# Reciprocal roots on GpSimd, a variance from the first moments, and two of a batch's query/key products one iteration earlier

## What is computed

```
x = x + Attn(norm(x))            # 16 heads of 32; softmax(q k^T); product with Wff, plus bff
x = x + CrossAttn(ctx, norm(x))  # one head of 512 over 750 context rows
h = norm(x); x = x + gate * agg  # agg: 8 best of 2048 keys, softmax, weighted sum of gathered rows
norm(x) = (x - mean) / sqrt(var + 1e-5)
v    = var of the normalised rows h;   lv = log1p(v)
gate = sigmoid(gwc * clip(0.5 * lv / mean(lv) + 2.5 * sigmoid(mlp(h)), 0, 5) + gbc)
```

## Time and profile before

| | |
|---|---|
| time, median of 3 runs | 2811.0 us (2810.16 to 2812.33) |
| profiled execution: span from first to last instruction | 2786.2 us |
| the profiled execution's own time | not given beside its span; the runs' median is 24.8 us above it |
| PE busy, share of the span | 2556.4 us, 92% |
| DVE, ACT, POOL busy | 77%, 51%, 25% |
| TensorE's granted clock, mean over the span | 0.971 |
| loads and stores of HBM | 358.87 MB, mean 129 GB/s |

### The profile page before, as it was taken

How to read it: one execution, slowest core, us unless ns; L and a number is a source line. 1 busy time by engine, 2 the same in 40 slices (tenths; PEclk the granted TensorE clock), 3 DMA queues, 4 the chain that set the end, 5 groups by cost and what they waited for, 6 DMA issues and landing times.

```text
span 2786.2 us, 56938 instructions
## 1 busy us (share of the span) xinstructions
PE 2556.4 (92%) x19090; PEld 2104.0 (76%) x19090; DVE 2146.0 (77%) x4207; ACT 1431.3 (51%) x4247; POOL 683.1 (25%) x650
## 2 busy tenths in 40 slices
PE   6899999999999999999999999999999999999730
PEld 4578878887888788878887888778888887788520
DVE  5456888888888888888888888888888888887552
ACT  2345554555555545555555455555554555555252
POOL 0001222222222222222222222222222222222254
PEclk9899999999999999999999999999999999999955
DMA  5223354454544444444444445444445454444799
GB/s 189 53 80 80 107 132 121 128 137 130 133 121 112 130 125 123 138 131 131 128 111 128 131 113 138 131 131 131 115 126 134 106 139 130 132 130 111 202 205 178
DMA packets 131542, 358.87 MB, mean 129 GB/s; under 512 B 21906, under 2 KB 26514, under 8 KB 123267
## 3 DMA queue, kind: packets, MB, share of 16 engines
q0 software_dynamic: 63520, 160.60, 24.4%
q1 hardware_dynamic: 63188, 192.15, 23.6%
q10 hardware_dynamic: 4784, 5.46, 0.6%
HBM read 316.37 MB, written 41.78 MB: 129 GB/s over the span
## 4 chain that ended last, share of the span: by engine, by line
PE 74%; DVE 8%; ACT 7%; issue 7%; DMA 2%; POOL 1%; DVEq 0%; ACTq 0%; POOLq 0%; SPq 0%
PE psX L1144 43%; PE psA L1144 13%; PE psA L1153 5%; PE psF L1144 4%; PE psA L1210 4%; DVE top L999 3%; PE psA L1233 2%; ACT paT L640 2%; PE psX L1153 2%; ACT sc L640 1%; DMA vg<-in_L_ffn_aux_values,idx 1%; ACT xT_hi L663 1%; DVE xmax L948 1%; PE psF L1153 1%; DVE idx L1002 1%
## 5 line engine op out<-in xcount | busy, mean ns | idle before, releaser
L589 POOL DMA_INDIRECT vg<-in_L_ffn_aux_values,idx x512 | 491.7, 960 | 1550.5 <-DVE agg L1028 1053.8
L684 ACT ACTIVATE pa<-psA,nmax 112x224 f32<-112x224 f32 x1024 | 444.6, 450 | 197.8 <-DVE nmax L917 194.5
L917 DVE TENSOR_REDUCE nmax<-psA 112x4 f32<-112x896 f32 x256 | 267.1, 1085 | 100.9 <-PE psA L1210 100.9
L1144 PE MATMUL psX<-big,gT 128*112 128x375 f32 x1024 | 333.4, 478 | 0.6 <-ACT gT L711 0.6
L1028 DVE SCALAR_TENSOR_TENSOR agg<-vg,wt,agg 112x512 f32<-112x512 f32 x406 | 303.8, 748 | 9.2
L1144 PE MATMUL psX<-pT,cx 125*128 125x224 f32 x1536 | 299.1, 355 | 0.0
L1144 PEld LDWEIGHTS psX<-pT,cx 125*128 125x128 f32 x1536 | 288.0, 190 | 4.0 <-issue 0.3
L932 DVE TENSOR_TENSOR pa<-pa,rsum 112x896 f32<-112x896 f32 x256 | 279.4, 1091 | 8.8
L1144 PEld LDWEIGHTS psX<-big,gT 128*112 128x112 f32 x1024 | 175.2, 176 | 126.0 <-issue 0.9
L1153 PE MATMUL psA<-ident,pa 112*112 112x112 f32 x2048 | 227.2, 262 | 19.5 <-DVE oT_lo L895 19.4
L640 ACT COPY paT<-psA 112x448 f32<-112x448 f32 x512 | 237.2, 560 | 11.4 <-PE psA L1153 9.4
(11 more groups left out here) (220 smaller groups left out, 5957.0 us busy)
## 6 DMA issues: line engine op xcount, KB each, us to landing
big<-in_ctx_t SPq DMA_DIRECT2D x32, 1500.0 KB, 8.1
cx<-in_ctx SPq DMA_DIRECT2D x32, 1344.0 KB
xa<-in_x SPq DMA_DIRECT2D x64, 224.0 KB
centered<-in_x_t SPq DMA_DIRECT2D x32, 448.0 KB, 4.6
x<-in_L_attn_bff POOLq DMA_DIRECT2D x32, 448.0 KB, 5.7
x<-cb_scratch POOLq DMA_DIRECT2D x32, 448.0 KB, 5.9
x<-in_x SPq DMA_DIRECT2D x31, 448.0 KB
out<-x SPq DMA_DIRECT2D x30, 448.0 KB, 3.1
```

Source lines behind the costliest of these rows:

```text
L589: pool.indirect_dma_start(vg[:, c % SLOTS, k, :], None, aux_values, bass.IndirectOffsetOnAxis(ap=idx[:, t, n:n + 1], axis=0))\
L684: last = nc.scalar.activation(pa[:, t, h, :], psA[0:R, h, t * S:(t + 1) * S], ACT.Exp, bias=nmax[:, k % 2, h, t:t + 1], accum_out=rsum[:, ...
L917: nc.vector.tensor_reduce(nmax[:, k % 2, h:h + 2, :], psA[0:R, h:h + 2, 0:T * S].rearrange("p h (t s) -> p h t s", t=T), AX_X, ALU.max, ne ...
L1144: last = nc.tensor.matmul(dst, stationary, moving, start=n == 0, stop=n == len(pairs) - 1)
```

## The change

Four edits, of which only the order of steps touches TensorE.

1. Roots. The seed and the three Newton rounds are gone from VectorE. A new step `root`, right after the new step `stat`, lets GpSimd raise `ve` to the power -0.5 in one instruction. VectorE's `norm` waits for it, and in N SyncE's store does. One constant tile is set at the start.
2. Variance. The second statistics of F are gone. GpSimd multiplies the first variance by the root twice, after `add_base`, with a wait between; ScalarE's logarithm waits for `var_taken`.
3. Split entry. `enter` is two steps, one for each tile. They stand next to each other everywhere.
4. Order. `qk` 0 and 1 of the next batch (stream Q) stand at the end of an iteration, around `mix` 3; `G sum` 0 is now ahead of `score` 0, N's and F's statistics stand ahead of `score` 1, `share` 1 ahead of `X score` 0, and `X prob` 0 ahead of `mix` 0. In `SETUP` the indices move by two, since two A steps fewer stand ahead.

```diff
-    ("A", "qk", 0), ("A", "qk", 1), ("A", "score", 0), ("G", "sum", 0), ("A", "share", 0), ("X", "enter", 0),
...
+    ("G", "sum", 0), ("A", "score", 0), ("A", "share", 0), ("X", "enter", 0), ("X", "enter", 1), ("A", "value", 0),
+    ("X", "stat", 0), ("X", "root", 0), ("X", "norm", 0), ("G", "sum", 1), ("A", "qk", 2), ("G", "sum", 2),
+    ("X", "turn", 0), ("A", "prob", 0), ("X", "query", 0), ("F", "stat", 0), ("F", "root", 0), ("F", "norm", 0),
+    ("N", "stat", 0), ("N", "root", 0), ("N", "spread", 0), ("A", "score", 1), ("F", "turn", 0), ("G", "sum", 3),
+    ("A", "share", 1), ("X", "score", 0), ("A", "qk", 3), ("X", "score", 1), ("N", "center", 0), ("F", "route", 0),
+    ("X", "prob", 0), ("A", "mix", 0), ("G", "sum", 4), ("A", "prob", 1), ("F", "learn", 0), ("X", "prob", 1),
...
+    ("A", "prob", 3), ("R", "load", 0), ("F", "score", 3), ("F", "top", 1), ("Q", "qk", 0), ("A", "mix", 3),
+    ("Q", "qk", 1), ("R", "bias", 0),
...
-         ("W", "keys", 1),)
-SETUP = {1: (("W", "keys", 2),),
+         ("W", "keys", 1), ("Q", "qk", 0), ("Q", "qk", 1), ("W", "keys", 2))
+SETUP = {0: (("W", "keys", 3),),
...
-                batch = {"N": i + 1, "A": i, "R": i, "X": i - 1, "F": i - 2, "G": i - 3, "W": 0}
+                batch = {"N": i + 1, "Q": i + 1, "A": i, "R": i, "X": i - 1, "F": i - 2, "G": i - 3, "W": 0}
...
-                sp.wait_ge(steps["N"], N_STEPS * (b + 1))
+                sp.wait_ge(rooted["N"], b + 1)
...
                 nc.gpsimd.tensor_tensor(dst[:, :, :], x2[:, :, :], xnf[:, :, :], ALU.add).then_inc(base_ready, 1)
+                nc.gpsimd.tensor_tensor(var_part[:, :], mv["F"][:, :, 1], rstd["F"][:, :], ALU.mult).then_inc(var_step, 1)
+                pool.wait_ge(var_step, b + 1)
+                nc.gpsimd.tensor_tensor(columns(var_all, b), var_part[:, :], rstd["F"][:, :], ALU.mult).then_inc(var_taken, 1)
+
+            def norm_root(s):
+                def step(b, _):
+                    pool.wait_ge(steps[s], per_batch[s] * b + MOMENTS)
+                    if s == "N":
+                        wait(pool, moments_stored, 16 * b)
+                    apart(pool)
+                    nc.gpsimd.tensor_tensor(rstd[s][:, :], ve[s][:, :], power[:, :], ALU.pow).then_inc(rooted[s], 1)
+                return step
...
             def norm(s, b, src, dst, normed):
-                statistics(s, b, src, rstd[s][:, :])
+                dve.wait_ge(rooted[s], b + 1)
```

More of the change, by code:

```diff
@@ L28 @@
 F32R = mybir.dt.float32r
-I32 = mybir.dt.int32
 U32 = mybir.dt.uint32
@@ L109 @@
          ("A", "mix"): 1,
-         ("X", "enter"): 2, ("X", "turn"): 2, ("X", "query"): 2, ("X", "score"): 2, ("X", "prob"): 2,
+         ("X", "enter"): 1, ("X", "turn"): 2, ("X", "query"): 2, ("X", "score"): 2, ("X", "prob"): 2,
          ("X", "mix"): 1, ("X", "out"): 1,
          ("F", "turn"): 2, ("F", "route"): 1, ("F", "learn"): 1, ("F", "score"): 2}
-EXTRA_PREC = ((("N", "norm", 0), ("F", "turn", 0)), (("N", "norm", 0), ("X", "prob", 0)), (("X", "enter", 0), ("N", "center", 0)),
+EXTRA_PREC = ((("N", "stat", 0), ("F", "turn", 0)), (("N", "stat", 0), ("X", "prob", 0)), (("X", "enter", 1), ("N", "center", 0)),
               (("N", "center", 0), ("A", "mix", 0)))
-FIRST = (("N", "norm", 0), ("N", "spread", 0), ("W", "mean", 0), ("N", "center", 0), ("W", "split", 0),
+FIRST = (("N", "stat", 0), ("N", "root", 0), ("N", "spread", 0), ("W", "mean", 0), ("N", "center", 0), ("W", "split", 0),
          ("W", "mean", 1), ("W", "mean", 2), ("W", "split", 1), ("W", "split", 2), ("W", "keys", 0),
-         ("W", "keys", 1),)
-SETUP = {1: (("W", "keys", 2),),
[7 rows of a table removed]
+         ("W", "keys", 1), ("Q", "qk", 0), ("Q", "qk", 1), ("W", "keys", 2))
+SETUP = {0: (("W", "keys", 3),),
[6 rows of a table added]
 FILL = {}
 JOBS = {"A": 0, "X": 0, "F": 0}
-for _s, _step, _arg in ORDER:
+for _s, _step, _arg in (("A", "qk", 0), ("A", "qk", 1)) + ORDER:
     if (_s, _step) in FILLS:
@@ L231, in build @@
         rstd = {s: sb(f"rstd_{s}", [R, T]) for s in "NXF"}
-        tmp = {s: sb(f"tmp_{s}", [R, T]) for s in "NXF"}
+        power = sb("power", [R, T])
+        var_part = sb("var_part", [R, T])
         var_all = sb("var_all", [R, B * T])
@@ L538, in _ @@
                           ("W", "cb"): first_cxT, ("W", "gb"): first_ctx,
-                          ("X", "score"): next_cxT, ("X", "mix"): next_ctx, ("N", "norm"): store_moments,
+                          ("X", "score"): next_cxT, ("X", "mix"): next_ctx, ("N", "root"): store_moments,
                           ("N", "spread"): spread_moments, ("N", "center"): next_xt, ("X", "enter"): entered, ("R", "load"): next_xr,
@@ L610, in _ @@
             pool.wait_ge(small_loaded, 16 * SMALL)
-            pipeline(pool, {("Z", "scale"): add_scaled,  ("R", "bias"): bias_x, ("X", "norm"): bias_x1, ("F", "norm"): add_base,
+            pipeline(pool, {("Z", "scale"): add_scaled,  ("R", "bias"): bias_x, ("N", "root"): norm_root("N"), ("X", "root"): norm_root("X"), ("F", "root"): norm_root("F"), ("X", "norm"): bias_x1, ("F", "norm"): add_base,
                             ("G", "sum"): next_gather, ("F", "top"): first_gather})
@@ L804, in _ @@
                            ("W", "split"): split_hi, ("W", "wff"): wff_hi_half, ("W", "m2"): m2_hi_half, ("N", "center"): center_hi, ("A", "mix"): mixed,
-                           ("A", "qk"): qk, ("A", "value"): value, ("A", "score"): exp_scores, ("A", "prob"): probs_turned,
+                           ("A", "qk"): qk, ("Q", "qk"): qk, ("A", "value"): value, ("A", "score"): exp_scores, ("A", "prob"): probs_turned,
                            ("X", "turn"): turn("X", "turn", xnxT), ("X", "query"): query,
@@ L833, in statistics @@
                 apart(dve)
+                if s == "F":
+                    wait(dve, var_taken, b)
+                    apart(dve)
                 for t in range(T):
@@ L880, in f_norm @@
                 norm("F", b, x2, xnf, x2_normed)
-                dve.wait_ge(x2_normed, b + 1)
-                for t in range(T):
-                    last = nc.vector.bn_stats(stats["F"][:, t, :], xnf[:, t, :])
-                mark("F", last)
-                settle("F", b)
-                apart(dve)
-                for t in range(T):
-                    last = nc.vector.bn_aggr(mv["F"][:, t, :], stats["F"][:, t, :])
-                mark("F", last)
-                settle("F", b)
-                mark("F", nc.vector.tensor_copy(columns(var_all, b), mv["F"][:, :, 1]))
             def lo(dst, src, hi):
@@ L935, in share, with x_enter @@
                 assert k < NB - 1 or count["A"] == A_STEPS
-            def x_enter(b, _):
-                dve.wait_ge(xr_biased, 16 * (b + 1))
-                for t in range(T):
-                    j = FILL["X", "enter", 0] + t
-                    wait_full(dve, "X", j, b)
-                    nc.vector.tensor_tensor(x1[:, t, :], bank("X", j)[0:R, :], x1[:, t, :], ALU.add)\
-                        .then_inc(drained["X"][j % banks["X"]], 1)
+            def x_enter(b, t):
+                if t == 0:
+                    dve.wait_ge(xr_biased, 16 * (b + 1))
+                j = FILL["X", "enter", t]
+                wait_full(dve, "X", j, b)
+                nc.vector.tensor_tensor(x1[:, t, :], bank("X", j)[0:R, :], x1[:, t, :], ALU.add)\
+                    .then_inc(drained["X"][j % banks["X"]], 1)
             def x_maxima(b, t):
@@ L1235, in mixed, with enter @@
                 filled("A", j, last)
-            def enter(b, _):
-                if isinstance(b, int) and b == 0:
-                    pe.wait_ge(wff_split, 1)
-                    pe.wait_ge(setup_drained, FILLED)
-                wait_drained(pe, "A", FILL["A", "mix", NB - 1], b)
-                for t in range(T):
-                    j = FILL["X", "enter", 0] + t
-                    wait_free(pe, "X", j, b)
-                    filled("X", j, product3(bank("X", j)[0:R, :], [(both(oT, ALL, c, slice(t * R, (t + 1) * R)), both(wffT, ALL, c, ALL))
-                                                                   for c in range(C)]))
+            def enter(b, t):
+                if t == 0:
+                    if isinstance(b, int) and b == 0:
+                        pe.wait_ge(wff_split, 1)
+                        pe.wait_ge(setup_drained, FILLED)
+                    wait_drained(pe, "A", FILL["A", "mix", NB - 1], b)
+                j = FILL["X", "enter", t]
+                wait_free(pe, "X", j, b)
+                filled("X", j, product3(bank("X", j)[0:R, :], [(both(oT, ALL, c, slice(t * R, (t + 1) * R)), both(wffT, ALL, c, ALL))
+                                                               for c in range(C)]))
             def query(b, _):
```

52 lines of the change are left out of this document (24 added, 28 removed), and 54 rows, old and new, of tables (LAST, ORDER, SETUP).

## The result

The changed kernel takes **2901.5 us** (2900.9 to 2907.5, 4 runs) where the kernel before takes 2810.7 on the same chip: ratio 1.0323, 95% interval 1.0311 to 1.0336. 2822 with a range of 2798 to 2848 was predicted: the sign was right, the size was not, by 79.5 us, and the time lies above the range.

A forecast was written before the change was run, and what follows sets the result against it. TensorE, 92% busy, was taken to bound the kernel. Steady iterations' +10.2 and the start's +0.8 gave +11.0 on a span of 2786.2 with 24.8 around it (median 2811.0): 2822 us, range 2798 to 2848.

The forecast's parts named there:

- Part 1: qk products around mix 3: wait ahead of score stays 1.43 us; worth 0 in steady iterations.
- Part 2: X prob 0 ahead of mix 0: prob 1's transposes wait 0.84 instead of 0.51 us, 31 times, +10.2 us.
- Part 3: Roots moved to GpSimd: power assumed 0.5 us (0.1 to 2.4), costing 0 up to 1.0.
- Rival A: Slow GpSimd power, over 1.0 us, delays iterations through VectorE's queue: 2837 us at 1.5, 2863 at 2.4; chance 0.2.
- Part 4: Start: first root held by small loads, +9.5 us; waits and half clock won back, -8.7; net +0.8.
- Part 5: Variance products on GpSimd and split entry: 0, bounds -2.4 to +2.4 us.
- B: VectorE's relief reaches the prob 1 wait and removes its whole 0.51 us: 2796 us; chance 0.14.
- C: Wait ahead of prob 1's transposes stays 0.51 us, start and loss cancel: 2812 us; chance 0.2.

The follow-up runs named there:

- the roots alone: Kernel before in its old order, with roots and variance on GpSimd and the split entry: ratio 1.0028, 2790.8 us.
- the version with the first root ahead: Changed kernel with G sum 5 behind F score 1, X prob 0 behind mix 0, GpSimd's first root before its small-loads wait: 2803.5 us, ratio 0.9976.
- qk version: Kernel before with only the four qk products moved around mix 3 and weight preparation at the changed kernel's places: 2810.1 us, ratio 1.0002.
- G sum 5 back: Changed kernel with G sum 5 and its gathers moved behind F score 1: ratio 1.0091 and 1.0068 on kind I, 1.0028 on kind II.
- kernel before with G sum 5 early: Kernel before with only G sum 5 moved ahead of F score 0: 2847.9 us, ratio 1.0239 on kind I.

## Why the prediction missed

**Part 1, the qk products: right.** The wait ahead of `score` is 1.4 each, 46.7 in 33, the same row as before, and the move alone measures 1.0002.

**Part 2, X prob 0 ahead of mix 0: right in its direction, too small in its size.** The wait of `prob` 1 went from 0.51 to 1.09, not to 0.84. The failing clause is "VectorE's own pT copy fits ahead of it". The timeline of the changed kernel (it answers rows 5): oT_hi moves behind pT by a step of 0.32, as forecast; but VectorE's copy of pT, 0.51 long, starts at 1170.17 and ends at 1170.68. By the hand-over of rows 5 (0.22) oT_lo could start at 1170.51, and it starts at 1170.71. These two are 0.52 of the 0.58; the rest was not traced to a row. The wait is the same on both kinds of chip.

```profile
1169.26 0.45 ACT L765 ACTIVATE sc<-psF,b1c 128x224 f32<-128x224 f32 x1
1169.61 0.43 ACT L660 COPY pT<-psX 125x336 f32<-125x336 f32 x1
1169.93 0.36 ACT L721 CAST oT_hi<-psA 128x224 fp32r<-128x224 f32 x1
1170.17 0.51 DVE L956 COPY pT<-psX 125x336 f32<-125x336 f32 x1
1170.71 0.39 DVE L898 TENSOR_TENSOR oT_lo<-psA,oT_hi 128x224 fp32r<-128x224 f32 x1
1171.15 0.40 PE L1156 MATMUL psA<-ident,pa 112*112 112x112 f32 x2 [1.09 <-DVE oT_lo L898]
```

An iteration is 80.14 on kind I instead of 79.37. Of these 0.77, 0.58 are this wait; the other 0.19 lie in PE's busy time and were not traced to a row. 31 times 0.77 is 24 us, where the prediction had 10.2. That is the whole of the 1.0075 there: the medians are 2807.9 and 2784.8, 23.1 apart.

**Part 3, the roots: right.** The page, part 5, has the power at 0.70 to 0.74 us, between the assumed 0.5 and the 1.0 up to which it was to cost nothing; it costs the iterations nothing (the roots alone leave them at 79.4). Rival A is out. By the Trainium skill, GPSIMD Engine Reference, section 2.1 (Instruction dispatch), the first call of a fresh kernel pays some 6 us; the first power of the start takes 0.73 and SyncE's store follows it by 0.02. In the version with the first root ahead it starts 0.19 us behind the end of `ve_N` on VectorE (10.93 against 10.74). So this case does not show it. (In the prediction, 2822 and 5.95 make 2828, not 2829.)

```profile
L599 POOL TENSOR_TENSOR rstd_F<-ve_F,power 112x2 f32<-112x2 f32 x32 | 23.5, 735 | 4.9 <-DVE ve_F L859 4.1
```

**Part 4, the start: right in its net.** The first root is held by the small loads until 23.98 (27.1 was assumed, from rows 9), and `centered` comes at 32.6 instead of 25.56: 7 us later, where 9.5 (35.1) was forecast. The 3.5 wait of iteration 0 is gone, and the half clock behind it too. But an earlier stretch of half clock has grown (from 37 to 51 us in this trace, from 39 to 46 in that of before), so the 4 us counted for the clock were not won in full. The first Wff matmul of the changed kernel is at 130.2 to 133.2 in three traces, of the kernel before at 131.4 and 134.4. The net is 0 within that spread; +0.8 was forecast.

```profile
23.98 0.73 POOL L599 TENSOR_TENSOR rstd_N<-ve_N,power 112x2 f32<-112x2 f32 x1 [20.03 <-DMA gbc<-in_L_ffn_gate_bias]
24.73 0.35 SPq L476 DMA_DIRECT2D moments_scratch<-rstd_N  x1
...
32.61 1.09 DVE L903 TENSOR_TENSOR centered<-centered,spread 128x896 f32<-128x896 f32 x1 [21.73 <-DMA spread<-moments_scratch]
```

**Part 5: right**, 0.21 us for each product, hidden.

**The sum: wrong, in two places.** First, "span 2786.2 and 24.8 around it, which is the median's 2811.0" took for a constant what was none: 2 us lie around a span, and the other 23 are the difference between a trace of one kind of chip and the runs of the other. That difference was a sign of a cost absent from the trace, and it was waved through as an offset. Second, a term that is missing, and this is the step that fails: the prediction lets the steady iterations grow by part 2 alone and puts the move of `G sum` 5 and its gathers at nothing. On kind II PE's posts for `score` 2 are held beside these gathers, 3.1 to 3.3 us instead of 0.2 to 0.3. On that kind the kernel before pays about 26 us (2810.7 against 2784.8), and the changed kernel about 88 (2895.6 against 2807.9), 62 more. With the 24 of the iterations that is the 85.5 (2895.6 - 2810.1) and, within 5, the 90.8 of the result. In the trace of the result an iteration is 83.6 against 80.14 on kind I: 2.5 us longer in every one, by the wait for the held posts and what follows from it, and 1.5 to 2.3 more in the 13 in which the clock fell. The prediction kept the clock of a steady iteration at full. What moved is `G sum` 5: it frees the last buffers, its gathers start with `score` 2's end instead of behind it, and the prediction looked at G's first steps in part 3 but never asked where the transfers of the later ones would fall.

No rival met it: A (slow power) comes nearest, with 2863, by a mechanism that did not happen. B and C are out, since the `prob` 1 wait grew.

**What is shown and what isn't.** Shown: on kind II no late posts without gathers; with them 3.1 us and more at `score` 2 with G sum 5 early, none there with it back; on kind I none in either. Not shown: why PE's posts are held, what differs between the chips and whether it stays with a chip, whether moving GpSimd's issue alone is enough, and why the clock falls in some iterations and not in others with the same wait. The kernel before was not traced on kind II, so its 26 us are read from the qk version's trace (ratio 1.0002). Also, on kind II some events near gathers are missing from the record (of the changed kernel 14,492 of DMAs against 16,410 on kind I). So a post counts here as held only where the instruction that waits for it starts late too.

## What to carry to other kernels

Before a sum is built on a trace, its span must account for the median of the runs; a gap of 0.9% can be a cost that the trace doesn't hold, and one that the change will multiply. A step that is moved takes its transfers along: write down which matmuls end during each gather that GpSimd issues, and keep releases on which the path depends out of it. A wait of PE can cost more than its length: here waits of 1.5 to 1.8 us were followed by half clock in a third to a half of the iterations. And an experiment is to be read beside the unchanged and the changed kernel on the same chip: here "G sum 5 back" looked like the cure on a chip that had no illness.

## What the runs showed of the hardware

- Two kinds of chip by the same kernel: 2783 to 2785.7 and 2808.5 to 2811 us. The changed kernel without GpSimd's indirect DMAs takes 2775 to 2777 on both.
- On the second kind a post of PE that falls into a running gather (0.93 us long) can be held. Counted from the start of the last matmul, it came after 3.0 to 3.3 us where one gather began with that matmul and another followed at 1.23; after 1.0 or 1.7 instead of 0.2 to 0.3 at `score` 2 of the qk version, where a gather began 0.3 to 0.4 before; and some 0.3 late at `mix` 1 of the version with G sum 5 back. Not every one is held: X score's posts, 0.34 behind the start of a gather, come after 0.49, as on the first kind. VectorE's posts go on in such a time: the one for oT_lo, in the timeline of the result, comes 0.01 after its end at 1175.59, inside a gather.
- TensorE's granted clock fell to half right behind a wait of PE of 1.7 to 1.8 us in 13 of 27 steady iterations (changed kernel, kind II), and behind one of 1.5 us in 9 of 27 (kernel before with G sum 5 early, kind I). Such an iteration is 1.5 to 2.3 us longer. In the trace of before and of the changed kernel on kind I, where the longest wait of a steady iteration is 1.44 us, it stayed full in all of them.
- A power of two columns on GpSimd takes 0.70 to 0.74 us, a product 0.21.
